# Two staging buffers for rotated blocks, an earlier place for the copies and the reciprocals' spreading, and a sum kept in PSUM, in a two-layer transformer kernel

## The reference

```python
q_mid = rmsnorm(hidden_states @ q_a_w.T, q_a_ln_w)
q = (q_mid @ q_b_w.T).reshape(b, s, H, D_Q).transpose(0, 2, 1, 3)
q_nope, q_pe = (q[..., :D_NOPE], q[..., D_NOPE:])
q_pe = apply_rope(q_pe, cos, sin)      # x * cos + rotate_half(x) * sin
k_pe = apply_rope(k_pe, cos, sin)
scores = jnp.einsum('bhqd,bhkd->bhqk', qf, kf) * scale
probs = jax.nn.softmax(scores.astype(jnp.float32), axis=-1).astype(dt)
ctx = jnp.einsum('bhqk,bhkd->bhqd', probs, v)
main_out = ctx.transpose(0, 2, 1, 3).reshape(b, s, H * D_V) @ o_w.T
```

## Time and profile before

| what | value |
|---|---|
| median of 3 runs | 1342.91 us (1338.31 to 1346.03) |
| the profiled execution's own time | 1350.24 us |
| its span | 1348.4 us |
| PE busy, share of the span | 1199.9 us, 89% |
| DVE busy | 890.0 us, 66% |
| ACT busy | 651.6 us, 48% |
| POOL busy | 534.3 us, 40% |
| mean granted PE clock | 0.964 |
| mean of ACT's 48 copies to the staging tile (L1603) | 0.592 us |

### The profile page before, as it was taken

How to read it: one execution, slowest core, us unless ns; L and a number is a source line. 1 busy time by engine, 2 the same in 40 slices (tenths; PEclk the granted TensorE clock), 3 DMA queues, 4 the chain that set the end, 5 groups by cost and what they waited for, 6 DMA issues and landing times. The chain is left out here.

```text
span 1348.4 us, 34624 instructions
## 1 busy us (share of the span) xinstructions
PE 1199.9 (89%) x14433; PEld 842.0 (62%) x14436; DVE 890.0 (66%) x1354; ACT 651.6 (48%) x1242; POOL 534.3 (40%) x531
## 2 busy tenths in 40 slices
PE   8999999997787887888878878899998898899998
PEld 5644444475666665666666656788864344678997
DVE  4789988176666767676767685745677764565655
ACT  3479888833333333333433342433244767435553
POOL 4256265235565747574747403445200000331221
PEclk8989999999899989989999898999999999899999
DMA  7780010011111111111111203011042510101110
GB/s 275 191 172 2 1 28 9 7 45 28 29 30 31 30 30 30 30 30 30 30 29 26 65 11 132 6 48 48 11 124 53 117 37 1 32 9 34 54 40 32
DMA packets 41699, 66.25 MB, mean 49 GB/s; under 512 B 8476, under 2 KB 27676, under 8 KB 40604
## 3 DMA queue, kind: packets, MB, share of 16 engines
q1 hardware_dynamic: 41544, 64.04, 17.4%
HBM read 45.60 MB, written 8.45 MB: 40 GB/s over the span
## 5 line engine op out<-in xcount | busy, mean ns | idle before, releaser
L1818 DVE TENSOR_REDUCE nmq<-bank 128x1 f32<-128x1024 f32 x128 | 153.0, 1195 | 108.6 <-PE bank L1811 108.3
L1833 ACT ACTIVATE P<-bank,nmq 128x1024 f32<-128x1024 f32 x128 | 142.8, 1116 | 166.4 <-DVE nmq L1818 165.7
L1913 PE MATMUL bank<-PT,kv 32*64 32x128 f32 x7936 | 150.3, 296 | 62.5 <-ACT t L1603 46.1
L1456 ACT ACTIVATE Pb<-bank 128x512 f32<-128x512 f32 (+3 forms) x355 | 180.7, 573 | 31.7 <-PE bank L1435 11.1
L1913 PEld LDWEIGHTS bank<-PT,kv 32*64 32x64 f32 x7936 | 132.2, 143 | 89.4 <-issue 89.1
L1306 DVE TENSOR_REDUCE mp<-bank 128x2 f32<-128x1024 f32 x128 | 153.5, 1222 | 29.8 <-PE bank L1298 29.1
L1846 DVE STREAM_TRANSPOSE PT<-P 128x1024 f32<-128x1024 f32 x124 | 151.5, 1222 | 0.0
L1809 PE MATMUL bank<-qk1h,qk0h 128*128 128x512 f32 x256 | 113.7, 444 | 6.7 <-ACT P L1833 5.2
L1377 DVE TENSOR_REDUCE mpc<-bank 128x2 f32<-128x1024 f32 (+2 forms) x96 | 88.3, 954 | 43.1 <-PE bank L1365 22.1
L1478 PE MATMUL bank<-Pb,vx 128*17 128x256 f32 (+3 forms) x1222 | 106.3, 408 | 0.7 <-ACT OTa L1492 0.5
L1810 PE MATMUL bank<-qk1l,qk0h 128*128 128x512 f32 x256 | 102.9, 402 | 0.0
(11 more groups left out here) (354 smaller groups left out, 2921.0 us busy)
## 6 DMA issues: line engine op xcount, KB each, us to landing
t<-t SPq DMA_DIRECT2D x128, 64.0 KB, 2.0
wr<-wf SPq DMA_DIRECT2D x25, 256.0 KB, 2.7
wraw<-wf SPq DMA_DIRECT2D x8, 768.0 KB, 4.4
scratch<-stgr SPq DMA_DIRECT2D x4, 1024.0 KB, 4.0
Rs<-shares SPq DMA_DIRECT2D x64, 64.0 KB, 2.8
scratch<-stg SPq DMA_DIRECT2D x8, 384.0 KB, 2.6
qst<-scratch SPq DMA_DIRECT2D x9, 256.0 KB, 8.2
owT<-owT SPq DMA_DIRECT2D x1, 2048.0 KB, 11.4
```

What stands on the lines that cost most here:

```text
L1456: e.activation(PBR[l][i % len(PBR[l])][:, 0:c], bank[b][:, 0:c], ACT.Exp, scale=0.25).then_inc(exp_ok[0], 1)
L1818: e.tensor_reduce(nmq[:, n % 8:n % 8 + 1], scores(u, i), AX, ALU.max, negate=True).then_inc(mp_ok, 1)
L1833: e.activation(probabilities(u, i)[:], scores(u, i), ACT.Exp, bias=nmq[:, n % 8:n % 8 + 1], accum_out=sums[:, u % 2, i:i + 1]).then_inc(ex ...
L1913: last = e.matmul(rest[64 * c:64 * c + 64, g, 64 - 64 * c:192 - 64 * c], kv4[b % 4][rows, b // 4, :], transposed(u, b)[rows, :], start=(b ...
```

## The change

Four things change, in one diff:

- There are two staging tiles instead of one. The second lies where `kvT` was, so that its first copy waits for the last reader of `kvT` (`key_lo`). From pair 1 on, block `k` takes tile `k % 2`, and the copy of a block waits for the block two before it. The second tile's swaps count on the semaphore `d_below`.
- In the list, `("spread", u - 1)` now stands right behind `("rec", u - 1)`, and the copy of a unit's second prepared block stands ahead of `("expo", u, 1)` instead of behind it.
- SP issues a block's swap at `("pcopy", p, k)` and no longer at `("prep", p, k)`.
- In `dve_weigh` the crossed sum is written back into PSUM in place, and the multiplication reads it there and writes `OTm`. The wait for the projection before (`pr_mm`), which reads `OTm`, moves to the second instruction.

```diff
-        order.extend([("rec", u - 1), ("vturn", u - 1, 3), ("expo", u, 0)])
+        order.extend([("rec", u - 1), ("spread", u - 1), ("vturn", u - 1, 3), ("expo", u, 0)])
         prep(4 * u, "pcopy")
...
         prep(4 * u + 1, "prep")
-        order.extend([("spread", u - 1), ("vturn", u, 0), ("expo", u, 1)])
         prep(4 * u + 1, "pcopy")
+        order.extend([("vturn", u, 0), ("expo", u, 1)])
...
-    t12 = M0.sb("t12", [128, 2, 512], F32)
+    t12 = [M0.sb("t120", [128, 2, 512], F32), sb("t121", [128, 2, 512], F32, at=KVT)]
...
+    def staging(p, k):
+
+        return t12[k % 2 if p else 0]
+
+    def staged_before(p, k):
+
+        m = len(FIRST) * p + k
+        back = 2 if m > len(FIRST) + 1 else 1
+        return None if m in (0, len(FIRST) + 1) else divmod(m - back, len(FIRST))
...
     def act_product(e, p, k):
         kind, r = FIRST[k]
         e.wait_ge(rp_mm if kind == "rope" else lt_mm, prepared(kind, p) + r + 1)
-        if p or k:
-            had, of = FIRST[k - 1], p if k else p - 1
+        if (p, k) == (1, 1):
+            e.wait_ge(key_lo, 4)
+        elif staged_before(p, k) is not None:
+            of, n = staged_before(p, k)
+            had = FIRST[n]
             done = prepared(had[0], of) + had[1] + 1
             if had[0] == "rope":
                 e.wait_ge(rp_cos, done)
-                e.wait_ge(d_sw, 64 * done)
+                e.wait_ge(*SWAPS[of, n])
             else:
                 e.wait_ge(lt_lo, done)
...
-        by_row = OTm[:].rearrange("p (j g q) -> p j g q", j=2, g=4)
-        e.tensor_tensor(by_row, rest[:, :, 64:128].rearrange("p g (j q) -> p j g q", j=2),
-                        other[:].rearrange("p g (j q) -> p j g q", j=2), ALU.add).then_inc(sum_ok, 1)
-        e.wait_ge(sum_ok, SUM0 + u + 1)
-        e.wait_ge(d_spread, 32 * (u + 1))
-        e.tensor_tensor(OTm[:], OTm[:], Rs[:, u % 2, :], ALU.mult).then_inc(ot_ok[1], 1)
+        both = rest[:, :, 64:128]
+        e.tensor_tensor(both, both, other[:], ALU.add).then_inc(sum_ok, 1)
+        e.wait_ge(sum_ok, SUM0 + u + 1)
+        e.wait_ge(d_spread, 32 * (u + 1))
+        if u:
+            e.wait_ge(pr_mm, u)
+        by_row = "p (j g q) -> p j g q"
+        e.tensor_tensor(OTm[:].rearrange(by_row, j=2, g=4), both.rearrange("p g (j q) -> p j g q", j=2),
+                        Rs[:, u % 2, :].rearrange(by_row, j=2, g=4), ALU.mult).then_inc(ot_ok[1], 1)
...
         for s in MAIN:
-            if s[0] == "prep":
+            if s[0] == "pcopy":
                 sp_swap(e, s[1], s[2])
```

More of the change, by code:

```diff
@@ L107, in main_order @@
     output(30)
-    order.extend([("rec", 31), ("vturn", 31, 3), ("turn", 0), ("spread", 31), ("pv", 31, 0), ("pv", 31, 1), ("hT", 0),
+    order.extend([("rec", 31), ("spread", 31), ("vturn", 31, 3), ("turn", 0), ("pv", 31, 0), ("pv", 31, 1), ("hT", 0),
                   ("wup", 1), ("wdown", 1), ("lift", 31), ("ot", 31), ("project", 31), ("logits", 0), ("add", 31)])
@@ L1590, in prepared @@
         return (4 if kind == "rope" else 2) * p
+    def staging(p, k):
[4 more added lines that the diff above has]
+        return None if m in (0, len(FIRST) + 1) else divmod(m - back, len(FIRST))
+    SWAPS, swapped_ = {}, [0, 32]
+    for p_, k_ in itertools.product(range(8), range(len(FIRST))):
+        if FIRST[k_][0] == "rope":
+            z_ = k_ % 2 if p_ else 0
+            swapped_[z_] += 64
+            SWAPS[p_, k_] = ((d_sw, d_below)[z_], swapped_[z_])
     def act_product(e, p, k):
@@ L1599, in act_product @@
                 e.wait_ge(rp_cos, done)
-                e.wait_ge(d_sw, 64 * done)
+                e.wait_ge(*SWAPS[of, n])
             else:
                 e.wait_ge(lt_lo, done)
-        e.activation(t12[:, 0, :], bank[PREP[p, k][0] if p else BANK_P0[k][0]][:], ACT.Copy).then_inc(pc_ok, 1)
+        e.activation(staging(p, k)[:, 0, :], bank[PREP[p, k][0] if p else BANK_P0[k][0]][:], ACT.Copy).then_inc(pc_ok, 1)
     def sp_swap(e, p, k):
@@ L1609, in sp_swap @@
         e.wait_ge(pc_ok, len(FIRST) * p + k + 1)
-        if p or r:
-            e.wait_ge(rp_sum, 4 * p + r)
+        before = staged_before(p, k)
+        while before is not None and FIRST[before[1]][0] != "rope":
+            before = staged_before(*before)
+        if before is not None:
+            e.wait_ge(rp_sum, prepared("rope", before[0]) + FIRST[before[1]][1] + 1)
+        t = staging(p, k)
         for q in range(4):
-            e.dma_start(t12[32 * (q ^ 1):32 * (q ^ 1) + 32, 1, :], t12[32 * q:32 * q + 32, 0, :]).then_inc(d_sw, 16)
+            e.dma_start(t[32 * (q ^ 1):32 * (q ^ 1) + 32, 1, :], t[32 * q:32 * q + 32, 0, :]).then_inc(SWAPS[p, k][0], 16)
     def pool_product(e, p, k):
@@ L1624, in pool_product @@
                 e.wait_ge(rp_lo, r)
-            e.tensor_tensor(Rt[:], t12[:, 0, :], cosT[:, cs], ALU.mult).then_inc(rp_cos, 1)
-            e.wait_ge(d_sw, 64 * (r + 1))
-            e.tensor_tensor(t12[:, 1, :], t12[:, 1, :], sinT[:, cs], ALU.mult).then_inc(rp_sin, 1)
+            e.tensor_tensor(Rt[:], t[:, 0, :], cosT[:, cs], ALU.mult).then_inc(rp_cos, 1)
+            e.wait_ge(*SWAPS[p, k])
+            e.tensor_tensor(t[:, 1, :], t[:, 1, :], sinT[:, cs], ALU.mult).then_inc(rp_sin, 1)
             e.wait_ge(rp_cos, r + 1)
             e.wait_ge(rp_sin, r + 1)
-            e.tensor_tensor(Rt[:], Rt[:], t12[:, 1, :], ALU.add).then_inc(rp_sum, 1)
+            e.tensor_tensor(Rt[:], Rt[:], t[:, 1, :], ALU.add).then_inc(rp_sum, 1)
             e.wait_ge(rp_sum, r + 1)
@@ L1634, in pool_product @@
             n, cs = 0, cols(part)
-            src, tops, hi, lo = t12[:, 0, :], (0, 1), lt_hi, lt_lo
+            src, tops, hi, lo = t[:, 0, :], (0, 1), lt_hi, lt_lo
         if k == 0:
```

## The result

| | before | changed |
|---|---|---|
| median | 1344.47 us of 4 runs (1338.31 to 1349.66) | 1308.56 us of 4 runs (1305.52 to 1313.86) |
| ratio, 95% interval | | 0.9742 (0.9704 to 0.9779) |
| profiled execution | 1350.24 us | 1305.70 us |
| mean granted clock | 0.964 | 0.971 |

The change makes the kernel 2.6% faster, 36 us by the medians. The forecast of 1298 us is 10.6 us too low, and the time lies in its range.

A forecast was written before the change was run, and what follows sets the result against it. PE, 89% busy, idled on the copy and weighing; afterwards the SP-POOL loop binds at 59.6 us, plus 1.2 lost. Seven rounds give 42 us, plus 2.3 ahead, 44.3 us: 1298 us against the 1342.91 median, range 1278 to 1322.

The forecast's parts named there:

- The copy's wait: PE's `pv` waiting for ACT's copy into `t` in main attention: 20 waits, all hidden, nominal gain 46.1 us.
- The weighing: DVE's 32 multiplications before the projection: delay beside POOL goes when one operand is in PSUM, gain 9.7 us.
- the rule that speaks against the edit: DVE's PSUM source has fixed cost 120 cycles against SBUF's 58, an estimated 2.1 us over 32; forecast took nothing.
- The spreading: Four DVE multiplications waiting for `Rs`: spreading right behind the small DMAs lands it before use, gain 7.8 us.
- The loop through SP and POOL: PE's two units, DVE, SP's spreading, R1's swap and POOL through Q0 bind a round at 59.6 us, against PE's 53.3.
- The wait for `wql`: PE's R2 matmuls wait 3.5 us a round for the q weights' low part: 20.1 us chain against PE's 16.6.
- The time lost beside the waits: PE's loss at lower clock and between instructions, 4 us a round before; forecast added 1.2 us to the loop.
- The rival *slower: PE's new POOL waits each bring a half-clock stretch costing 2 us; round 69.5 us, time 1360 us; chance 0.04.
- What a round saves: Main attention, four units a round: 66.8 us falls to 60.8, saving 6.0 us.
- Seven equal rounds: Main attention: seven rounds each save the same 6.0 us, 42 us together.
- The rival *PE-bound: POOL's loop does not bind main attention; a round is 57.3 us, time 1274 us; chance 0.10.
- nominal 63.6 us: Copy, weighing and spreading gains taken alone, 46.1 + 9.7 + 7.8 us; not expected in full, as PE would outrun POOL.

The follow-up runs named there:

- the two edits together: Changed kernel with PREP_AT = (4, 5, 8, 9, 12, 16) and the q weights' load and split at the end of the pair before; 1277.24 us, ratio 0.9505.

## Why the prediction was right, and where it was off

- **The copy's wait.** Right: 46.1 us gone from the list. The two runs that split it show that the two tiles alone leave 31.9 us of it, and that with all of the change but the copy's new place 26.2 us are left. The new place without the second tile was not run.
- **The weighing.** Right, and settled by a run of its own: 9.8 us of DVE's time against 9.7 forecast, 6.4 us of the kernel's. (The long one at 351.21 ended 0.28 us behind POOL's instruction, not one normal duration, 0.43 us, as the prediction reads it.) For the rule that speaks against the edit (the Trainium skill, VectorE: DVE Perf Modes, The TRN2 errata) the trace shows nothing with a PSUM source: 424 ns. The sum with its result in PSUM takes 8 ns more than before (432 or 433 against 425), 0.3 us in all; the upper bound of 13 us was far off.
- **The spreading.** The 7.8 us went as forecast, and so did the price: "it stood ahead of the small DMAs". The run with the spreading late shows that the price is larger than the gain. The forecast had both numbers, 7.8 us won here and 44 instead of 63.6 us won overall, and didn't set them against each other.
- **The loop through SP and POOL.** Right that POOL's lateness would take back part of the gain, and at which two places: the late spreading and the two edits together show it. The loop is also sized well: 59.6 us forecast, and from the score block at 328.45 to Q0's low part at 388.45 there are 60.0, in the next four rounds 60.0 to 61.8. But PE is not held by its end. For Q0 the forecast had seven waits of 2.8 us, and there is one, of 5.15 us in the last round, since PE, held longer at `wql`, comes to the score block later. What sets the other rounds is PE's own path with the wait for `wql` in it, and the run with R1's and R2's swaps early, 3 us lower instead of 8 to 30, bears that out.
- **The wait for `wql`.** The forecast had seven waits of 3.5 us, and there are seven of 4.7 (32.6 us). From the multiplication's end to `wql` it had 20.1 us, and there are 21.75 (344.04 to 365.79). Of its pieces, from that end to the swap's issue it had 8.1 us (3.4 + 3.2 + 1.5) and there are 8.08 (344.04 to 352.12), and from the sine product to `wql` 8.1 against 8.02. **The mis-sized term is the landing of R0's swap.** The forecast took R1's 3.9 us for it. R1's is right (365.43 to 369.43, 4.0 us), but R0's takes 5.65 us to the sine product where POOL itself is the last to come, and where POOL waits for the swap 4.6 to 5.4 us (5.36 from 414.43 to 419.79). The trace of before had R0's own figure: 4.62 us to the sine product at 364.73, and 4.5 to 5.8 us in its seven pairs, 5.0 in the mean. With 5.0 the forecast's sum gives a wait of 4.6 us.

```profile
360.11 3.09 SPq L1613 DMA_DIRECT2D t<-t  x4
```

- **The time lost beside the waits.** Taken as 1.2 us a round, as most dips of the clock would go with their waits. The new waits are 5 us long and bring their own: in the four middle rounds 53.3 us of PE's work, 4.95 us of waits for `wql` and 0.16 for Q1 are 58.4 us, and such a round takes 62.0, so 3.6 us are lost. The rival *slower* had this mechanism (2 us for each new wait), and it works at a smaller scale: in a unit 4p+2 the 14.0 us of work and 5.24 us of wait leave 2.9 us of the 22.2.
- **What a round saves.** 6.0 us forecast, 5.8 us measured in the four middle rounds. The agreement hides the slip in the count of units: the round before takes 67.8 us, not 66.8, and the round after 62.0, not 60.8; both were a microsecond too short. Over all seven the round before takes 68.7 us. Held against that, the forecast's round of 60.8 would have given 58 us in all and 1285 us, 24 us too low. So the slip and the round that was sized too short made up for each other in good part, which is luck.
- **Seven equal rounds.** Wrong: 42 us forecast, 35.2 measured. The first gives 9.0 us and the last costs 3.3. With the 4.4 us ahead of them, where 2.3 were forecast, the stage gives 39.6 us of the 44.3; the rest of the miss lies between these two executions and the medians. In the last round PE waits 2.75 us for `wql` and 5.15 for Q0. Besides, ACT splits expert weights that POOL has to have scaled, a step that the change doesn't touch. The rows are POOL's, ACT's and PE's of the changed kernel:

```profile
729.09 1.26 POOL L2282 TENSOR_TENSOR wraw<-wraw,gab 128x512 f32<-128x512 f32 x1
730.38 0.63 ACT L2288 ACTIVATE wh<-wraw 128x512 fp32r<-128x512 f32 x1 [4.14 <-POOL wraw L2282]
...
732.16 0.72 PE L1834 MATMUL bank<-qk1h,qk0h 128*128 128x512 f32 x1 [3.13 <-ACT P L1858]
```

  POOL, late from the round before, holds ACT for 4.14 us. The exponential stands behind that on ACT's queue, and PE waits 3.13 us for it. Before, the same score block waited 1.09 us. In the repeated run of the changed kernel PE waits only 0.87 us for Q0 in this round, but ACT 6.33 us for POOL and PE 5.31 us behind it, and the round takes 69.5 us. In the kernel with earlier places and weights ACT doesn't wait there, and the last round takes 56.5 us. So it goes with POOL's lateness. The forecast looked at who waits for POOL on PE alone and not on ACT. No run changed this step alone.
- **The rival *PE-bound*** (57.3 us a round by the short count, 1274 us) is what the kernel with earlier places and weights shows, 57.2 us by the same count (59.2 by whole rounds) and 1277 us: it is the state of the kernel once POOL is early, and the changed kernel isn't in it.

So of the nominal 63.6 us, the medians show 36. Against the rest stand 38.1 us of new waits for POOL, with a lower clock behind the longer ones, at places to which PE came too early.

## What to carry to other kernels

When waits are taken off the busiest engine, add up the loop that feeds it (here reciprocals, SP's issues, a swap's landing, POOL's work) from the trace, and compare it with what is left of the engine's own round. Add to that round the new waits that it meets inside, each with the time lost behind it: here that path, not the loop, set the length. Take each link of a chain from its own rows, as two swaps of the same size landed after 3.9 and 5.0 us. A wait that appears at a new place is a symptom if removing it alone moves it on: two edits that each gain nothing alone may win 31 us together. On a queue that takes its DMAs in order, don't put a DMA that waits for another's landing ahead of those that a slow engine needs next, even if it is a little late itself.

## What the runs showed of the hardware

- Around a wait of PE of 5.24 us (360.8 to 366.05) the granted clock is 0.50 from 364 to 370, and the matmuls of 512 columns there take 0.63 us instead of 0.40. With the long waits gone, in the kernel with earlier places and weights, the mean over seven rounds is 0.99.
- A DVE sum of 128x256 in fp32 takes 432 ns with its result in PSUM and 425 with it in SBUF, and a multiplication with a PSUM operand 424 ns, never over 426 beside POOL. With both operands in SBUF it took up to 1528 ns.
- SP takes 2.5 to 3.8 us to issue the four DMAs of R0's swap, in both kernels (3.09 us at 360.11 before, 3.22 us at 352.12 now).
